# A fused preactivation conv kernel: image 1's first convolution started ahead, set-up work moved between engines, and the second convolution's groups moved one chunk up

## The reference

```
x: 8 images, 32 channels, 128 x 128, float32
def gn(v): per image and channel, (v - mean) / sqrt(var + 1e-5)
x  = x + G @ (pw @ (A @ depthwise3x3(gn(x))))        # A, G: row softmax of 32 x 32 weights
y  = gn(x)
off = conv3x3(y, w_off)                              # 2 offsets a pixel and channel
xd = bilinear sample of y at (row + off_r, col + off_c), clipped to the image
x  = x + conv3x3(xd, w_conv) + b_conv
```

## Time and profile before

| | us |
|---|---|
| median of 3 runs (lowest, highest) | 858.96 (858.32, 861.0) |
| the profiled execution | 857.73 |
| its span, first to last instruction | 855.8 |
| mean granted TensorE clock | 0.95 |
| busy: PE, DVE, POOL, ACT | 739.6, 542.5, 483.3, 445.4 |

### The profile page before, as it was taken

One profiled execution on the slowest core, in us unless ns is written; L12 is line 12 of the kernel. 1 busy time (PEld: TensorE's weight loads), 2 busy tenths in 40 slices (PEclk: granted clock), 3 DMA queues, 4 the chain that ended last, 5 costly groups with the idle time before them and its releaser, 6 DMA issues. The chain is left out here.

```text
span 855.8 us, 9271 instructions
## 1 busy us (share of the span) xinstructions
PE 739.6 (86%) x2780; PEld 291.2 (34%) x2780; DVE 542.5 (63%) x1076; ACT 445.4 (52%) x792; POOL 483.3 (56%) x411
## 2 busy tenths in 40 slices
PE   2866499399999989999899999899989999919994
PEld 2422133133433334333333333333333333303431
DVE  6365257946896289754995299745994585534661
ACT  0112476466655385466554584556565655464630
POOL 0001366676468566664668467664668469546960
PEclk9988699789999999999999999999999999969997
DMA  8298445659946986589957995689867444691454
GB/s 148 56 170 135 95 81 108 140 115 172 182 103 152 166 183 121 130 187 164 187 115 168 158 197 106 144 183 171 156 128 175 99 98 100 160 211 28 103 129 117
DMA packets 216455, 118.52 MB, mean 138 GB/s; under 512 B 142576, under 2 KB 208208, under 8 KB 212304
## 3 DMA queue, kind: packets, MB, share of 16 engines
q1 hardware_dynamic: 186768, 104.24, 59.0%
q10 hardware_dynamic: 29632, 13.64, 10.1%
HBM read 16.91 MB, written 16.78 MB: 39 GB/s over the span
## 5 line engine op out<-in xcount | busy, mean ns | idle before, releaser
L1145 DVE COPY_PREDICATED other_row<-down_ps,row_diff 128x768 f32<-128x768 int32 x128 | 123.4, 1016 | 223.4 <-ACT down_ps L793 223.4
L953 POOL TENSOR_TENSOR other_row<-other_row,x_quads 128x512 f32<-128x512 f32 x64 | 76.1, 1189 | 246.0 <-DVE other_row L1157 245.5
L537 PE MATMUL c_ps<-xb,w 128*64 128x512 f32 (+1 forms) x432 | 192.1, 593 | 17.1 <-ACT xb L689 17.1
L539 PE MATMUL c_ps<-xa,w 128*64 128x512 f32 x432 | 198.2, 607 | 0.0
L632 PE MATMUL off_ps<-x1a,wo 128*128 128x512 f32 x384 | 190.1, 633 | 4.5 <-DVE other_row L1157 3.6
L537 PE MATMUL c_ps<-mapb,w 128*64 128x512 f32 (+1 forms) x336 | 152.4, 601 | 37.8 <-DMA mapb<-mapa 29.6
L632 PE MATMUL off_ps<-x1b,wo 128*128 128x512 f32 x384 | 175.4, 592 | 0.0
L539 PE MATMUL c_ps<-mapa,w 128*64 128x512 f32 x336 | 157.1, 615 | 0.0
L784 ACT ACTIVATE other_row<-row_diff 128x768 f32<-128x768 f32 x128 | 101.8, 844 | 86.6 <-POOL row_diff L939 67.1
L939 POOL TENSOR_TENSOR row_diff<-x_quads 128x594 f32<-128x594 f32 x64 | 79.2, 1239 | 84.6 <-ACT x_quads L818 84.6
L632 PEld LDWEIGHTS off_ps<-x1a,wo 128*128 128x128 f32 x384 | 70.1, 195 | 103.4 <-issue 92.0
(11 more groups left out here) (111 smaller groups left out, 810.0 us busy)
## 6 DMA issues: line engine op xcount, KB each, us to landing
xb<-xa SPq DMA_DIRECT2D x34, 520.0 KB, 6.5
x1b<-x1a SPq DMA_DIRECT2D x32, 520.0 KB, 6.4
mapb<-mapa SPq DMA_DIRECT2D x28, 520.0 KB, 7.7
mapa<-mapped SPq DMA_DIRECT2D x224, 64.0 KB, 2.3
out_dram<-x1a SPq DMA_DIRECT2D x52, 256.0 KB, 4.7
xa<-in_x_dram ACTq DMA_DIRECT2D x48, 256.0 KB, 7.3
x_quads<-x1a SPq DMA_DIRECT2D x178, 65.0 KB, 2.2
xa<-in_x_dram SPq DMA_DIRECT2D x16, 256.0 KB, 6.4
```

Of the source, the lines that this page charges most:

```text
L537: nc.tensor.matmul(bank[0:64, n0:4 * W], weights[:, kx, :], rows_b[:, b0:4 * g + 4, kx:kx + W], start=(kx == 0), stop=(kx == 2))
L539: last = nc.tensor.matmul(bank[64:128, :], weights[:, kx, :], rows_a[:, 4 * g:4 * g + 4, kx:kx + W], start=(kx == 0), stop=(kx == 2))
L953: step(pool.tensor_tensor(split(column), split(column), own, ALU.add))
L1145: last = dve.copy_predicated(other_row[n][:, :, KR // 2 * odd:KR // 2 * odd + KR // 2, :], bass.AP(tensor=rows.tensor, offset=rows.offset ...
```

## The change

In one edit:

- **Order.** Three groups of image 1's first convolution (`AHEAD`) run behind image 0's eight, before the offsets' bias; image 0's chunks 0 to 4 have one group each. In images 1 to 6 the second convolution of the image before has one group behind chunk 3, one behind chunk 4 and two behind 5, 6 and 7. Its groups come in another order, and only group number 2 waits for half 1 of `mapa` and `mapb`.
- **SP.** `mapb` half 0 is copied at the top of an image, before the store and the quads; `x1b` half 0 before the quads of half 0; the first half's store waits for seven additions; in the last image SP moves the quads of half 1, not ACT. The store of image 7's first half is issued by ACT.
- **Start.** `dw_w`, `off_w`, `conv_w` are loaded from ACT's queue; ACT makes the four-fold weight copies and `xb` of image 0, and writes `x1b` of image 0 straight from PSUM; POOL clears the base weights and does the 18 multiplies. x of image 1 is loaded into `x1a[2]` right after x of image 0 and copied into `mapb` (there being no map yet), and image 2's x goes to `xa` from SP. `w1`, `mean_x` and `bias_1` have two buffers. The transposed `conv_w` goes to `down_ps`, so the laying out is split (`lay_out_offsets`, `lay_out_conv2`).
- **Norms.** The mean is announced before the reciprocal root, not after. Image 1's x statistics and norm lie between image 0's x1 statistics. `x_stats(2, 0)` moves from chunk 5 to 3 and `x_stats(2, 1)` with the norm from 6 to 5 in image 0. ACT pads the map before chunk 0's parts instead of after them.

```diff
-    FIRST_CONV1 = [[], [0, 1], [2, 3], [4, 5], [6, 7], [], [], []]
+    AHEAD = [0, 1, 2]
+    FIRST_CONV1 = [[3], [4], [5], [6], [7], [], [], []]
     NEXT_CONV1 = [[0, 1], [2, 3], [4, 5], [6, 7], [], [], [], []]
-    LAST_CONV2 = [[], [], [], [], [0], [1, 2], [3, 4], [5, 6, 7]]
-    END_CONV2 = [[], [], [0], [1], [2], [3], [4], [5]]
-    CONV2_GROUPS = [0, 1, 4, 5, 2, 3, 6, 7]
-    STORE_AFTER = [6, 8]
+    LAST_CONV2 = [[], [], [], [0], [1], [2, 3], [4, 5], [6, 7]]
+    END_CONV2 = [[], [], [0], [1], [], [2], [3, 4], [5]]
+    CONV2_GROUPS = [1, 5, 0, 4, 2, 6, 3, 7]
+    STORE_AFTER = [7, 8]
...
-    NEXT_BIAS = 6
+    NEXT_BIAS = [7] + [6] * (NB - 1)
...
-    job_order = [("b1", 0, 0)] + [("x1", 0, m) for m in range(8)] + [("bo", 0, 0)]
+    job_order = [("b1", 0, 0)] + [("x1", 0, m) for m in range(8)]
+    job_order += [("b1", 1, 0)] + [("x1", 1, m) for m in AHEAD] + [("bo", 0, 0)]
...
+        def xa_of(i):
+            return x1a[2][:, 0:BL, :] if isinstance(i, int) and i == 1 else xa[:, :, :]
+        def xb_of(i):
+            return mapb[:, :, :] if isinstance(i, int) and i == 1 else xb[:, :, :]
...
             for half in range(2):
-                sp.wait_ge(xa_loaded[half], LOADS * DMA)
-                copy_xb(half)
-            sp.wait_ge(conv1_done, 5)
-            load_xa(sp, 1, 0)
-            sp.wait_ge(x1_ready, 5)
-            copy_x1b(0, 0)
-            sp.wait_ge(conv1_done, 8)
-            load_xa(sp, 1, 1)
+                sp.wait_ge(ahead_loaded[half], LOADS * DMA)
+                copy_xb(1, half, ahead_copied)
+            for hh in range(2):
+                sp.wait_ge(x1_ready, 3 + 4 * hh)
+                move_quads(sp, 0, 0, [hh])
             sp.wait_ge(x1_ready, 8)
-            copy_x1b(0, 1)
-            move_quads(sp, 0, 0)
             move_quads(sp, 0, 1)
...
                     sp.wait_ge(off_done, NK * i)
                     copy_x1b(i % 3, 1)
+                    sp.wait_ge(map_pads, i)
+                    sp.wait_ge(mapa_moved[0], A_MOVES * DMA * i)
+                    copy_mapb(0)
                 if nxt and i >= 2:
                     sp.wait_ge(out_ready, 8 * (i - 1))
-                    store(i - 2, (i - 2) % 3, 1)
+                    store(sp, i - 2, (i - 2) % 3, 1)
                 if prev:
                     sp.wait_ge(mapped_ready, NK * i)
-                    if nxt:
-                        move_quads(sp, i % 3, 1)
+                    move_quads(sp, i % 3, 1)
...
                     move_mapa(1)
-                    sp.wait_ge(map_pads, i)
-                    for half in range(2):
-                        sp.wait_ge(mapa_moved[half], A_MOVES * DMA * i)
-                        copy_mapb(half)
+                    sp.wait_ge(mapa_moved[1], A_MOVES * DMA * i)
+                    copy_mapb(1)
...
                 if nxt:
+                    sp.wait_ge(x1_ready, 8 * (i + 1) + 5)
+                    sp.wait_ge(off_done, NK * i + 4)
+                    copy_x1b((i + 1) % 3, 0)
                     sp.wait_ge(x1_ready, 8 * (i + 1) + 8)
                     sp.wait_ge(mapped_ready, NK * i + 5)
                     move_quads(sp, (i + 1) % 3, 0)
-                    copy_x1b((i + 1) % 3, 0)
...
             def conv2(i, wpar, m, ps):
-                if m == 0:
+                if m in (0, 2):
                     images = i + 1 if isinstance(i, int) else i
-                    for half in range(2):
+                    for half in [m // 2] if isinstance(i, int) else range(2):
                         pe.wait_ge(mapa_moved[half], A_MOVES * DMA * images)
                         pe.wait_ge(mapb_copied[half], B_MOVES * DMA * images)
...
+            for half in range(2):
+                b, e = half * HB, half * HB + HB
+                act.wait_ge(xa_loaded[half], LOADS * DMA)
+                act.activation(xb[0:2 * Q, b + 1:e + 1, 1:W + 1], xa[2 * Q:P, b:e, 1:W + 1], ACT.Copy)
+                act.activation(xb[2 * Q:P, b:e, 1:W + 1], xa[0:2 * Q, b:e, 1:W + 1], ACT.Copy)\
+                   .then_inc(xb_written, 1)
...
+                if isinstance(i, int) and i == 0:
+                    act.activation(x1b[0:2 * Q, 4 * m:4 * m + 4, 1:W + 1], rows[2 * Q:P, :, :], ACT.Identity,
+                                   bias=bias_1[bpar][2 * Q:P, :])
+                    act.activation(x1b[2 * Q:P, 4 * m - 1 + first:4 * m + 3, 1:W + 1], rows[0:2 * Q, first:4, :],
+                                   ACT.Identity, bias=bias_1[bpar][0:2 * Q, :]).then_inc(x1b_written, 1)
...
-                        if not nxt:
-                            act.wait_ge(mapped_ready, NK * i)
-                            move_quads(act, i % 3, 1)
...
+            act.wait_ge(out_ready, 8 * (NB - 1) + 6)
+            store(act, NB - 1, (NB - 1) % 3, 0)
...
             for m in range(NG):
                 x1_stats(0, 0, m)
+                if m < 2:
+                    x_stats(1, m)
+                if m == 2:
+                    x_norm(1, 1)
                 if m == 4:
-                    lay_out_l1_weights()
+                    lay_out_offsets()
             x1_norm(0, 0, 0)
-            for half in range(2):
-                x_stats(1, half)
-            x_norm(1)
+            lay_out_conv2()
+            for m in AHEAD:
+                x1_stats(1, 1, m)
```

More of the change, by code:

```diff
@@ L112, in deformable_preact_kernel @@
         w1_base = sb("w1_base", [P, 3, 2 * C])
-        w1 = sb("w1", [P, 3, 2 * C])
+        w1 = [sb(f"w1{n}", [P, 3, 2 * C]) for n in range(2)]
         wo_base = sb("wo_base", [P, 3, P])
@@ L292, in move_quads, with store @@
                                               1 + c0:1 + c1]).then_inc(quad_x1[half], DMA)
+        def store(queue, i, par, part):
+            image = out[i].rearrange("c (b r) w -> c b r w", r=4)
+            b, e = part * HB, part * HB + HB
+            for q in range(1, 4):
+                queue.dma_start(image[:, b:e, q - 1, :], x1a[par][Q * q:Q * q + Q, b:e, 1:W + 1])\
+                  .then_inc(stored[part], DMA)
+            b0, e0 = (1, HB) if part == 0 else (HB, BL)
+            queue.dma_start(image[:, b0 - 1:e0 - 1, 3, :], x1a[par][0:Q, b0:e0, 1:W + 1]).then_inc(stored[part], DMA)
+            if part == 0:
+                queue.dma_start(image[:, BL - 1:BL, 3, :], x1a[par][0:Q, BL:BL + 1, 1:W + 1])\
+                  .then_inc(stored[part], DMA)
         def split(tile):
@@ L300, in _ @@
         def _(sp):
[L301 to L305, removed]
+            sp.dma_start(soft_in[:, 0, :], att_w).then_inc(soft_load, DMA)
+            sp.dma_start(soft_in[:, 1, :], glob_w).then_inc(soft_load, DMA)
+            sp.dma_start(pw_sb, pw_w.rearrange("o c a b -> o (c a b)")).then_inc(l0_load, DMA)
             def wait_apart(sem_, value):
@@ L369, in store_end @@
                 sp.dma_start(image[:, b - 1:e - 1, 3, :], x1a[par][0:Q, b:e, 1:W + 1]).then_inc(stored[1], DMA)
[L371 to L384, removed]
-            for half in range(2):
-                load_xa(sp, 0, half)
+            for half in range(2):
+                load_x(sp, 0, half, xa_loaded)
+            for half in range(2):
+                sp.wait_ge(xa_loaded[half], LOADS * DMA)
+            for half in range(2):
+                load_x(sp, 1, half, ahead_loaded)
             for j in range(4):
@@ L678, in _ @@
         def _(act):
+            act.dma_start(w_off_sb, off_w.rearrange("o c a b -> o (c a b)")).then_inc(l1_load, DMA)
+            act.dma_start(w_conv_sb, conv_w.rearrange("o c a b -> o (c a b)")).then_inc(l1_load, DMA)
+            for j in range(4):
+                act.dma_start(dw_sb[Q * j:Q * j + Q, :], dw_w.rearrange("c o a b -> c (o a b)")).then_inc(l0_load, DMA)
             act.wait_ge(s_setup["dve"], 1)
@@ L682, in _ @@
                                      accum_out=soft_s[:, a:a + 1]).then_inc(s_setup["act"], 1)
+            act.wait_ge(l1_load, 2 * DMA)
+            for r in range(4):
+                act.activation(off_rep[:, :, r, :], w_off_sb.rearrange("p (c t) -> p t c", t=TAPS), ACT.Copy)
+                last = act.activation(conv_rep[:, :, r, :], w_conv_sb.rearrange("p (c t) -> p t c", t=TAPS), ACT.Copy)
+            last.then_inc(s_setup["act"], 1)
+            for half in range(2):
+                b, e = half * HB, half * HB + HB
[3 more added lines that the diff above has]
+                   .then_inc(xb_written, 1)
             def fill(rows, mean):
@@ L922, in _ @@
             pool.memset(xa[:, :, 0:WP:WP - 1], 0.0).then_inc(cleared, 1)
+            pool.wait_ge(s_setup["dve"], 5)
+            pool.wait_ge(l0_load, 5 * DMA)
+            pool.wait_ge(s_setup["pool"], 3)
+            pool.wait_ge(cleared, 1)
+            for rp in range(2):
+                for ky in range(3):
+                    j = rp + ky
+                    p = slice(Q * j, Q * j + Q)
+                    for kx in range(3):
+                        last = pool.tensor_scalar(w1_base[p, kx, C * rp:C * rp + C], mix_t[p, :],
```

(3 more changed lines are left out.)

257 lines of the change are left out of this document (143 added, 114 removed).

## The result

The changed kernel takes 816.62 us (median of 4 executions, 814.74 to 818.77) against 858.64 (856.6 to 861.0) of the kernel before on the same chip: ratio 0.951, 95% interval 0.948 to 0.955. Forecast: 811, range 794 to 828. Profiled, it took 817.38 with a span of 815.6, against 857.73 and 855.8: 40.2 us of span gone, where 47.0 were forecast.

A forecast was written before the change was run, and what follows sets the result against it. The prediction took TensorE (86% busy), idle at the ends, and a closed loop through SyncE in images 2 to 5 as bounds. 37.5 - 0.8 - 6.0 + 3.2 - 1.7 + 12.7 + 2.1 = 47.0 off 857.7: 810.7, forecast 811, range 794 to 828.

The forecast's parts named there:

- The start: Up to image 1's offset chunk 0 on TensorE: earlier x, groups ahead and earlier quads gain 37.5 us, bounds 25 and 42.
- The loop: Images 2 to 5: SyncE's closed loop sets the turn, which grows 1.5 to 97.0 us; four turns cost 6.0.
- the 3.0 I had credited: SyncE's loop: 5.3 us freed ahead of the store behind `mapa`, only 3.0 kept because it waits for the seventh addition.
- x of image i+2 disturbs the quads less: SyncE's loop: that x loads 2 to 3 us sooner, disturbing the last quads less; turn 97.0 instead of 97.3.
- The 95.3: Alternative turn in us if the 1.04 MB of `mapb` half 0 took 2.4 us at 436 GB/s; four turns cost nothing.
- The first c2 group: Second convolution's first group, now in chunk 3: waits of 2.2 us go, a bank wait of about 1.1 comes instead.
- Image 6: Without an x norm and set by TensorE, but with a later clamp: 91.6 us instead of 89.9, 1.7 lost.
- The end: Last image's offset chunk 0 to the last matmul: the 18.8 us wait goes, 12.7 us gained, bounds 4 and 17.
- SP issues them ... clamp of half 1 at + 24: Last image: SP instead of ScalarE issues 16 quads, with the half 1 clamp 24 us after its offset chunk 0 starts.
- T0 of image 5 to S6: Image 5's fifth `mapped` chunk to image 6's offset chunk 0: banks free sooner, 3.2 us gained once.
- the stores at the end: After the last matmul: one store goes out from ScalarE instead of SP, 2.1 us gained (0 to 3).
- image 1 up to its T0: Image 1 up to its fifth `mapped` chunk: 0.8 us longer, for the added addition ahead of the norm.

The follow-up runs named there:

- undone pieces: Three changed kernels, each with one piece of the start undone: no groups ahead 826.43 us, weights ahead of x 817.79, image 0's quads late 817.41.
- e9: The changed kernel with none of image 1's groups ahead of image 0's offsets; 826.43 us.
- e2: The changed kernel with the second store (half 1 of image i-2) issued behind the quads of half 1 instead of ahead; 797.76 us.
- e3: The changed kernel with the copy of `mapb` half 0 issued behind the quads of half 1 instead of ahead; 805.93 us.
- e4: The kernel before the change, with the store of half 1 of image i-2 moved behind the quads of half 1; 846.49 us.
- e6: The changed kernel with quads of half 1 first, then the second store, then `mapb` half 0; 790.67 us.
- e7: The changed kernel, in the last image alone: `mapb` half 0 behind the quads, image 6's first two c2 groups behind chunks 3 and 4; 810.88 us.
- e10: The changed kernel with image 2's x statistics behind chunks 1 and 2 of image 0 and its norm behind chunk 3; 818.02 us.
- e13: The changed kernel with dw_w, off_w and conv_w loaded from SyncE's queue ahead of x, as before the change; 817.79 us.
- e12: The kernel of e6 with both first c2 groups (second convolution) behind chunk 4; 786.97 us.
- e1: The changed kernel with both first c2 groups (second convolution) behind chunk 4; 823.17 us.

## Why the prediction was right, step by step

**The start (-38.0, forecast -37.5)** is nearly the whole gain, and its steps came within 2 us: convolution of image 0 at 25.3 (forecast 25.7), row differences 57.0 (58.3), S0 58.3 (59.6), VectorE on chunk 0 at 64.5 (65.8), chunk 4 done on TensorE at 96.0 (97.0), S1 133.9 (134.3). The undone pieces give 10.8 + 3.4 + 2.4 = 16.6 of it. The rest I take to be mostly image 1's x, which no longer waits for image 0's convolution: e9 and the kernel before differ by 19.9 at that one place. It was not taken out by itself, and the pieces need not add.

**The loop (+3.1, forecast +6.0).** That SyncE's loop sets the turn is shown by e2, e3, e4 and e6, which move only its members. Its terms, for T0 to the clamp, in the turn shown: the store behind `mapa` starts at T0 + 25.5, not + 23.4 (26.4 before), so of the 3.0 I had credited 0.9 came (2.1 in the turns where it starts at + 24.4); the stretch from there to the quads grew by 3.0 (16.77 for 13.73; 4.1 for `mapb` as forecast, a shorter store taking back 1); the quads' issue is 0.2 shorter; and from its end to the clamp it takes 3.8 instead of 5.8. I had named that last one (x of image i+2 disturbs the quads less) and allowed 0.3. The sum is 0 where I had 0.8: it came out near because two terms missed by about 2 us in opposite directions, which is luck. Clamp to the next T0 is 37.6 for 37.1 (38.1 in two of the four turns), where I had 0.7 for the added addition. The forecast also started from one turn of 95.5, and the four of before average 95.1. Five more kernels with the same steady loop (e7 to e10, e13) had turns of 95.05 to 95.8, before 95.1: the change costs a turn 0 to 0.8, not 1.5. The 95.3 that followed from the Trainium skill ("DMA: Bandwidth & Descriptors", Specifications) lies in that span, but not for its reason: the pair of `mapb` took 4.06 us of issue, by which it moved at 256 GB/s, near the 236 of the full queue of before, and not 2.4.

**The first c2 group** waited 2.3, not 1.1, with the lower clock for some 3 us behind it; in e12, where it doesn't stand there, three of four turns are 89.1 and not 89.7. It was not what set the turn of the changed kernel: e1 takes it away and its turns are longer. Image 6, which is TensorE's own, is where it was paid: + 2.6 instead of + 1.7. e2, e3 and e6, where the same wait is 0.93 and leaves the clock up, have 89.2 there for 92.5.

**The end (-6.3, forecast -12.7) is the term that was mis-sized.** I had said that a wait of TensorE over 5 us in the last image would refute my reading of it; there was one, of 6.92. The order of events was as written, and the 18.8 us wait for `mapb` did go. What failed is the step "SP issues them ... clamp of half 1 at + 24". The quads began at S7 + 11.4 and the clamp came 1.6 behind their last issue, so + 24 leaves 11.0 us for the sixteen, the price without other transfers, though two copies of 520 KB stood directly ahead of them in the same queue; it was 13.7 (the rows of before had 12.4 for quads of half 1 in a full queue). The clamp was 2.7 late, chunk 4 3.2, and from there GpSimd ran without a pause at 7.66 a chunk, so the delay reached the moved rows at the end. By e7 and e2, 2.5 of the 6.4 are the late clamp and 1.5 the clock that TensorE lost in its last wait, for which the forecast had no term. The other 2.4 I put down to GpSimd's rhythm, 7.66 where I had reckoned with 6.4 a chunk; no run changed it, so that is not shown.

**The rest.** T0 of image 5 to S6 gave 2.3 of 3.2, the stores at the end 1.1 of 2.1, and image 1 up to its T0 cost 1.9 for 0.8. These I did not look into. All terms together gave 40.2 us of span for 47.0.

## What to carry to other kernels

When an in-order queue of DMA issues sets the period of a loop, price each change by what stands ahead of the transfer that everybody waits for: here, moving two DMAs behind it was worth 1 to 2 us a turn, a store 3 to 4, both 5 to 6 (against 95.05 to 95.85 in the six kernels with the same loop). The order of another engine's work can have the opposite sign with the loop closed (e1, 6.5 slower) and open (e12, 3.7 faster in the medians), so open the loop first and tune the order after. When the same order gives other waits in another loop, as e1's bank waits that e12 doesn't have, the wait was a symptom. Two buffers between engines mean that work moved into an idle gap can starve the stage two chunks later.

## What was not expected of the hardware

- Four copies of 32 x 48 elements on VectorE took 0.80 us with GpSimd idle, 2.54 in the changed kernel's norm and 3.81 in e1's, where GpSimd was working on a chunk. Over the fourteen traces, the four copies took 0.80 to 0.86 us in the 42 norms where GpSimd was idle for most of them, and 1.8 to 3.9 in the 182 others. No experiment moved GpSimd's work away on purpose, so the cause is argued from this, not tested. Image 0's x norm took 6.3 us in all, image 2's, beside GpSimd, 8.3. The three rows are from the start and image 4 of the changed kernel, and from e1:

```profile
18.25 0.80 DVE L1138 COPY stats_c<-stats_x 32x48 f32<-32x48 f32 x4
...
472.31 2.54 DVE L1138 COPY stats_c<-stats 32x48 f32<-32x48 f32 x4
```
```profile
472.54 3.81 DVE L1138 COPY stats_c<-stats 32x48 f32<-32x48 f32 x4
```

- These copies reach into SyncE's loop. Where those of the x norm behind T0 took 2.75 to 2.78 us, the store that waits for the seventh addition started at T0 + 24.3 to 24.4, in all 37 such turns of the changed kernel and nine of its variants; in the three turns where they took 3.9 it started at + 25.5. In e1 they took 3.9 in every turn and the store came at + 26.1.

- Sixteen DMAs of 65 KB took SyncE 10.4 to 11.3 us to issue with little ahead of them and mostly 12 to 14.5 soon behind copies of 520 KB; a pair of those took 1.3 or 4.1. In these traces the same issue is priced by what the queue already holds.
